# A kept score made by one VectorE operation of two inputs and turned once, in place of a ScalarE part and a VectorE part turned twice

## The reference, cut to what matters

```python
xn = _rmsnorm(x, norm_w)
q = (xn @ w_q.T).reshape(b, t, H, 2, DK)              # H = 8 heads
sim1 = jnp.einsum('bthd,hkd->bthk', q[..., 0, :], keys[:, :, 0, :])   # 32 keys
sim2 = jnp.einsum('bthd,hkd->bthk', q[..., 1, :], keys[:, :, 1, :])
...
fs, pk = jax.lax.top_k(all_sc, K)                     # the 8 best of the sums s1 + s2
hidden = jax.nn.gelu(jnp.einsum('btd,bthkd->bthk', xn, wd), approximate=False)
hidden = hidden * jax.nn.relu(fs)
return jnp.einsum('bthk,bthkd->btd', hidden, wu)
```

## Time and profile before

| | us |
|---|---|
| median of 3 runs | 3211.59 |
| lowest and highest | 3202.09, 3213.86 |
| the profiled execution | 3200.05 |
| its span, first to last instruction | 3198.3 |
| mean granted TensorE clock | 0.869 |

### The profile page before, as it was taken

How to read it: one execution, slowest core, us unless ns; L and a number is a source line. 1 busy time by engine, 2 the same in 40 slices (tenths; PEclk the granted TensorE clock), 3 DMA queues, 4 the chain that set the end, 5 groups by cost and what they waited for, 6 DMA issues and landing times.

```text
span 3198.3 us, 41256 instructions
## 1 busy us (share of the span) xinstructions
PE 2715.7 (85%) x14161; PEld 1369.0 (43%) x14161; DVE 1759.3 (55%) x4863; ACT 1373.9 (43%) x3204; POOL 602.8 (19%) x849
## 2 busy tenths in 40 slices
PE   6898998889987888888879988987899788889885
PEld 3233335334543675244423333452345347732353
DVE  5535437645654687624565444476357548776154
ACT  2545622452324543564435556225532345335741
POOL 1220001220112672000013200003201138610000
PEclk9988998988878998869779888998898689988776
DMA  4000000000000000000100000000001000000000
GB/s 168 2 1 1 1 1 25 26 2 20 29 19 1 1 27 27 1 1 31 37 8 2 1 1 1 1 26 26 1 20 33 14 1 1 27 28 1 1 1 7
DMA packets 16432, 49.71 MB, mean 16 GB/s; under 512 B 1761, under 2 KB 8801, under 8 KB 14434
## 3 DMA queue, kind: packets, MB, share of 16 engines
q1 hardware_dynamic: 15650, 45.79, 4.1%
q10 hardware_dynamic: 576, 1.29, 0.1%
HBM read 45.43 MB, written 1.05 MB: 15 GB/s over the span
## 4 chain that ended last, share of the span: by engine, by line
PE 66%; DVE 17%; ACT 9%; issue 6%; POOL 1%; DMA 0%; SPq 0%; ACTq 0%; DVEq 0%; POOLq 0%
PE psum L582 5%; PE psum L2155 4%; PE psum L995 4%; PE psum L549 4%; PE psum L572 3%; PE psum L1006 3%; DVE floor_s L2254 2%; PE psum L979 2%; PE psum L1530 2%; PE psum L1822 2%; PE psum L1360 2%; PE psum L821 2%; PE psum L746 2%; ACT PT_s L648 2%; PE psum L1818 2%
## 5 line engine op out<-in xcount | busy, mean ns | idle before, releaser
L648 ACT ACTIVATE PT_s<-psum 128x512 f32<-128x512 f32 (+3 forms) x768 | 344.9, 497 | 277.7 <-PE psum L572 276.0
L396 POOL TENSOR_SCALAR ve<-mv 128x4 f32<-128x4 f32 x48 | 13.5, 281 | 1668.9 <-DVE mv L386 1668.7
L708 DVE CUSTOM_DVE_ANT_0 rest_s<-psum,packed_early 128x128 f32<-128x128 f32 (+3 forms) x512 | 226.6, 487 | 152.2 <-PE psum L555 150.1
L2181 POOL TENSOR_TENSOR buffer<-sim_s 128x1024 f32<-128x1024 f32 x128 | 271.7, 2138 | 171.7 <-DVE floor_s L2254 86.9
L572 PE MATMUL psum<-QS_s,KS_s 64*128 64x512 bf16 (+3 forms) x768 | 199.3, 364 | 36.1 <-DVE mx_s L708 16.6
L555 PE MATMUL psum<-KS_s,QS_s 64*128 64x512 bf16 (+3 forms) x768 | 186.9, 354 | 43.2 <-DVE mx_s L711 20.1
L582 PE MATMUL psum<-PT_s,vaug 128*9 128x512 f32 (+3 forms) x1536 | 179.4, 542 | 45.3 <-POOL PT_s L681 29.4
L681 POOL TENSOR_SCALAR_AFFINE_SELECT PT_s<-PT_s 128x128 f32<-128x128 f32 x512 | 146.0, 294 | 340.3 <-ACT PT_s L648 334.8
L711 DVE TENSOR_REDUCE mx_s<-psum 128x1 f32<-128x512 f32 x256 | 161.8, 683 | 83.7 <-PE psum L555 82.9
L1043 ACT ACTIVATE PT_s<-psum 128x512 f32<-128x512 f32 (+1 forms) x224 | 121.0, 592 | 164.4 <-PE psum L997 164.3
L2214 ACT ACTIVATE above_s<-buffer,below_s 128x1024 f32<-128x1024 f32 x128 | 145.2, 1149 | 96.6 <-POOL buffer L2181 58.0
(11 more groups left out here) (446 smaller groups left out, 5382.8 us busy)
## 6 DMA issues: line engine op xcount, KB each, us to landing
buffer<-packed_experts SPq DMA_DIRECT2D x36, 384.0 KB, 3.3
buffer<-packed_moe SPq DMA_DIRECT2D x4, 2048.0 KB, 8.2
buffer<-packed_cross SPq DMA_DIRECT2D x4, 2048.0 KB, 7.9
buffer<-packed_product SPq DMA_DIRECT2D x4, 1024.0 KB, 4.9
packed_early<-packed_early SPq DMA_DIRECT2D x1, 2654.5 KB
QS_s<-nmT_s SPq DMA_DIRECT2D x144, 4.0 KB
raw_s<-packed_setup SPq DMA_DIRECT2D x1, 1840.0 KB, 7.6
packed_late<-packed_late ACTq DMA_DIRECT2D x4, 314.0 KB, 3.7
```

The source lines that it names most:

```text
L648: a.activation(PT[:, u // 4 % 2, i, q0_of(c):T], bank[u % 3][:, q0_of(c):T], ACT.Exp, scale=scale).then_inc(exp_done.sem, 1)
L708: v.tensor_tensor_reduce(junk[:, u % 2, 0:w], bank[n % 4][:, 0:w], s.w["causal"][:, T - w:T], 1.0, -3e38, ALU.add, ALU.max, mx[:, j, h:h + ...
L2181: g.tensor_tensor(fs[:, n % 2], m[:, 0, :].unsqueeze(2).to_broadcast([P, NK, NK]), m[:, 1, :].unsqueeze(1).to_broadcast([P, NK, NK]), ALU. ...
```

## The change

ACT's part and the negative threshold go. DVE makes the kept score in one `scalar_tensor_tensor`, `(sum >= threshold) * sum`, which reads the tensor of sums as both of its tensor inputs. PE turns one tile of 1024 columns with 8 transposes where it turned two with 16. The ring has three tiles in place of two times two. POOL, PE and the copy of the similarities wait for `marked` alone.

```diff
-    KEPT = 2
+    KEPT = 3
...
-    below = s.tile("below9", [P, 2, NH])
...
-    above = s.tile("above9", [P, KEPT, NK * NK])
-    floor = s.tile("floor9", [P, KEPT, NK * NK])
+    kept = s.tile("kept9", [P, KEPT, NK * NK])
...
                 yield at(j, h) + 2.4
-                pe.wait_ge(*risen(n + 1))
                 pe.wait_ge(*marked(n + 1))
...
-                for i, rows in enumerate((above, floor)):
-                    for c in range(EC):
-                        mm = pe.matmul(CT[:, c * P:(c + 1) * P], rows[:, n % KEPT, c * P:(c + 1) * P], s.w["ident"][:], is_transpose=True,
-                                       start=(h == 0 and i == 0 and c % 4 == 0), stop=(h == NH - 1 and i == 1), skip_group_check=True)
+                for c in range(EC):
+                    mm = pe.matmul(CT[:, c * P:(c + 1) * P], kept[:, n % KEPT, c * P:(c + 1) * P], s.w["ident"][:], is_transpose=True,
+                                   start=(h == 0 and c % 4 == 0), stop=(h == NH - 1), skip_group_check=True)
...
                 if n >= 2:
-                    g.wait_ge(*risen(n - 1))
                     g.wait_ge(*marked(n - 1))
...
-                yield at(j, h) + 0.4
-                total, ready = sum_of(n)
-                a.wait_ge(*ready)
-                if h == 0:
-                    a.wait_ge(*limits_ready(j + 1))
-                if n >= KEPT:
-                    a.wait_ge(*added(n - KEPT + 1))
-                a.activation(above[:, n % KEPT, :], total, ACT.Relu, bias=below[:, j % 2, h:h + 1]).then_inc(risen.sem, 1)
...
-            link(v.tensor_scalar(thr[:, j % 2, :], best[:, :, 7], 0.0, None, ALU.max))
-            v.tensor_scalar(below[:, j % 2, :], thr[:, j % 2, :], -1.0, None, ALU.mult).then_inc(limits_ready.sem, 1)
+            v.tensor_scalar(thr[:, j % 2, :], best[:, :, 7], 0.0, None, ALU.max).then_inc(limits_ready.sem, 1)
+            v.wait_ge(*limits_ready(j + 1))
...
-            v.tensor_scalar(floor[:, n % KEPT, :], total, thr[:, j % 2, h:h + 1], thr[:, j % 2, h:h + 1], ALU.is_ge, ALU.mult).then_inc(marked.sem, 1)
+            v.scalar_tensor_tensor(kept[:, n % KEPT, :], total, thr[:, j % 2, h:h + 1], total, ALU.is_ge, ALU.mult).then_inc(marked.sem, 1)
```

More of the change, by code:

```diff
@@ L2082, in l2_ffn @@
     (chain, limits_ready, squares_ready, eps_added, inv_ready, xs_ready, xs_turned, xnT_ready, hidden_ready, gelu_ready, sim_ready, sim_copied, summed,
-     risen, marked, added, weighted, out_ready) = s.signals(
-        chain=1 + 4 * TJ, limits_ready=TJ, squares_ready=1, eps_added=1, inv_ready=1, xs_ready=TJ, xs_turned=1, xnT_ready=1, hidden_ready=EC, gelu_ready=EC,
-        sim_ready=TJ, sim_copied=TJ, summed=N, risen=N, marked=N, added=N, weighted=TJ, out_ready=TJ)
+     marked, added, weighted, out_ready) = s.signals(
+        chain=1 + 3 * TJ, limits_ready=TJ, squares_ready=1, eps_added=1, inv_ready=1, xs_ready=TJ, xs_turned=1, xnT_ready=1, hidden_ready=EC, gelu_ready=EC,
+        sim_ready=TJ, sim_copied=TJ, summed=N, marked=N, added=N, weighted=TJ, out_ready=TJ)
     s.new_stage()
@@ L2191, in copy_sim @@
             if j >= 2:
-                a.wait_ge(*risen(NH * (j - 1)))
                 a.wait_ge(*marked(NH * (j - 1)))
@@ L2205, in scalar @@
             for h in range(NH):
-                n = j * NH + h
-                yield at(j, h) + 0.4
-                total, ready = sum_of(n)
-                a.wait_ge(*ready)
-                if h == 0:
-                    a.wait_ge(*limits_ready(j + 1))
-                if n >= KEPT:
-                    a.wait_ge(*added(n - KEPT + 1))
-                a.activation(above[:, n % KEPT, :], total, ACT.Relu, bias=below[:, j % 2, h:h + 1]).then_inc(risen.sem, 1)
                 if h == 1 and 1 <= j < TJ - 1:
```

## The result

| | before | after |
|---|---|---|
| median of 18 runs | 3207.78 us | 3218.24 us |
| lowest and highest | 3196.30, 3217.56 | 3211.22, 3223.49 |
| the profiled execution | 3200.05 us | 3219.69 us |
| its span | 3198.3 us | 3218.0 us |

The ratio of the changed kernel to the one before is 1.0036, with a 95% interval of 1.0024 to 1.0048: 11.5 us slower, between 8 and 15. That is within the 0.5% named in the prediction, but clear of zero. With more runs the median of before came down from 3211.59 to 3207.78, so that the forecast of 3219 was met to a microsecond by a difference of 7 that should have been 11. That closeness is luck; the difference is what counts.

The account below looks back on a forecast made before the run. Shared stretches were taken as bound by DVE and POOL excluding each other, not by PE's transposes. The terms, 2 x (15 - 8.5 - 5.0 + 2) = +7 us, took the median from 3212 to 3219 us, range 3190 to 3244.

Parts of the forecast that it names:

- forecast case: Whole kernel: the forecast's own case, median 3219 us, 3203 to 3229, chance 0.50.
- lead: Part of each turn where stream 0 makes scores alone (1016 to 1101): forecast 8.5 us shorter.
- tail: Part of each turn with scores of stream 1 alone (1166 to 1256): forecast 5.0 us shorter.
- shared stretch: Part of each turn with scores of both streams (1101 to 1166): forecast 15 us longer, PE's saving giving nothing.
- clock: PE's clock falls in the shared stretch and the tail's first products pay: +2 us a turn, between 0 and 8.
- The exclusion: Shared stretch: the two-input DVE operation holds POOL up, 0.55 us more for each of 27 sums, 15 us.
- Rival C: Slower by TensorE's clock, low through the shared stretch into the tail: 8 to 10 us a turn, 3233, chance 0.20.
- A: Lead and tail: the transposes' 58 us go in full, as DVE isn't next; -26 us, 3186, chance 0.17.
- B: The new form doesn't exclude POOL, or runs at today's rate: -45 us, 3167, chance 0.05.
- D: Shared stretch: POOL is held for all of the operation's 1.22 us, +22 a stretch; +21, 3233, chance 0.08.
- ACT, the threshold and the ring: Dropping ACT's 147 us and the negative threshold, and a ring of three: all 0 outside one lead piece.

Follow-up runs that it names:

- e8: The changed kernel with only the scores of the shared stretch turned twice, their sum doubled; 3214.12 us, ratio 1.0037 to before.
- e4: The kernel before with the two-input operation as its VectorE part, ScalarE's part and 16 transposes kept; 3246.88 us, ratio 1.0109.
- e2: The changed kernel with a one-input VectorE copy of the sums, about as long, threshold left out; 3148.64 us, ratio 0.9798 to before.
- e3: The changed kernel with each kept score turned twice, 16 transposes a score, sum doubled; 3247.01 us, ratio 1.0112 to before.
- e1: The changed kernel with the one-input operation of before, 8 transposes, the part above the threshold left out; 3168.39 us, ratio 0.9865 to before.
- e7: e5 with an accumulator output on VectorE's shared-stretch operation, which then only compares, without multiplying by the threshold; 3174.74 us, ratio 0.9899 to before.
- e6: The changed kernel with a ring of two kept tiles in place of three; 3219.66 us, ratio 1.0034 to before.
- e5: The kernel before with the changed form for scores of lead and tail, the shared stretch's made as before; 3198.56 us, ratio 0.9969.

## Why the prediction was right, point by point

The forecast case came in: no gain, since what PE saves in lead and tail is outweighed by what DVE and POOL take from each other in the shared stretch. By its own steps, for a turn:

| step | forecast | measured |
|---|---|---|
| shared stretch | +15 | +14.0 |
| lead | -8.5 | -4.3 |
| tail | -5.0 | -3.0 |
| clock | +2, carried into the tail | 0 carried over (e8); what falls inside lead and tail is in their figures |
| sum | +3.5 | +6.7 |

The forecast named 76 and 85 us as the lead and the tail to come, and 76.7 and 85.4 were measured. That is no confirmation: the forecast took its steps from the rounded stretches of 85 and 90 us, the measured ones begin at 81.0 and 88.4. The steps came out at half and at six tenths of what was forecast.

*The exclusion* was right in mechanism and size. The price of 0.55 us a sum was taken from one row of POOL beside a two-input operation; it measured 0.53. That it is the exclusion and nothing else is shown from both sides: e4 puts the operation into the kernel before and gets +14.3 with everything else kept, but for an operation that is also longer; e2 tells length and exclusion apart: it takes the exclusion out of the changed kernel and gets -28.6 with the length of the operation nearly kept. That PE's saving is worth nothing there is shown by e3, 80.0 with twice the transposes.

*The lead* was mis-sized, above all in its DVE term. The two parts of the change can be put in one after the other, in either order. First the transposes (before, e1, after): halving them with the one-input operation gives 8.2 us, and the two-input operation then takes 3.9 back. First the operation (before, e4, e3, after): it costs 6.4, and halving the transposes then gives 11.3; ScalarE's part, the threshold and the ring make up the 0.6 between e4 and e3. The forecast had 10.9 for PE's side (7.0, 0.3, 1 and 2.6) and only 2.4 for the operation, as 0.41 us for each of six that stood on the chain. That price, the operation's length alone, is the step that was too small in both orders. With 8 transposes its length is worth 0.5 (e2 against e1), and the other 3.4 is the exclusion of POOL, which the forecast counted in the shared stretch alone: the changed kernel's lead is 3.4 longer than e2's, whose operation is 0.07 shorter and excludes nothing.

The clock in the lead was not foreseen either. Timeline of PE where stream 1's last projection runs, in the changed kernel and then before:
```profile
1059.69 0.39 PE L746 MATMUL psum<-packed_late,attT_s 128*128 128x128 f32 x2
1060.01 0.79 PE L748 MATMUL psum<-packed_row,ones 1*128 1x128 f32 x2
1060.73 0.80 PE L746 MATMUL psum<-packed_late,attT_s 128*128 128x128 f32 x2
...
1064.35 0.79 PE L748 MATMUL psum<-packed_row,ones 1*128 1x128 f32 x2
```
```profile
1062.18 0.39 PE L746 MATMUL psum<-packed_late,attT_s 128*128 128x128 f32 x2
1062.50 0.48 PE L748 MATMUL psum<-packed_row,ones 1*128 1x128 f32 x2
...
1064.99 0.48 PE L748 MATMUL psum<-packed_row,ones 1*128 1x128 f32 x2
```
The eight groups take 5.4 us after the change and 3.2 before: the granted clock is 0.5 from 1060.0 for 17.1 us, where before it fell only at 1070.9, for 6.8 us. Every kernel here with 8 transposes in the lead has this fall, 36 to 38 us into it. It doesn't need the shorter transposes: e3, with 16, has the groups in 5.7 us, wholly at 0.5, after a fall 43 us into its lead. In e4, the kernel before with nothing but the new operation, the clock is 0.5 for 3.4 us at 1028.6 and again at 1062.7; two turns of 16 transposes on the chain take 2.97 and 3.10 us in place of 1.94 and 1.94, and the groups 3.8. So about 2.7 of e4's 6.4 come by the clock (an estimate: these pieces less those of before), and there it fell with nothing changed but the operation. But e1, with the one-input operation and 8 transposes, has the long fall too. Either part of the change will do, then; what decides it was not tried.

*The tail* has the mechanism named, DVE next after PE. The 8 transposes with a one-input operation give 8.0 (e1); the two-input operation takes 5.0 back, 3.2 by its length and 1.8 by the exclusion (e2 lies between the two; that e1's operation excludes POOL a little too is left out of this split). The forecast let through 7.4 and took 2.4 back, and -3.0 is what was left: again the operation's price was too small. In the other order the operation costs 0.3 (e4) and the halving gives 2.3 (e3), so the parts don't add up independently here.

*Clock.* Rival C put the slower outcome on a low clock through the shared stretch. The clock did fall in the shared stretch, to 0.68 and 0.74, under the point named in one turn; but in the tail's first 20 us it was 0.76 and 0.83 (0.91 before), not under 0.7. In the shared stretch PE was busy for 63 and 59%, where the forecast said under half. The price of the low clock in that stretch was zero, 80.0 us at 0.68 and at 0.96 alike, and e8 has 0.76 at the start of the tail as well: what C held, that the low clock is carried over, is refuted. The tail's own fall stays, inside the -3.0, with its price open.

*The other rivals.* A, the transposes' time comes through (its sum has +2 for the clock where two turns make +4, which changes nothing here): not so. Even with the one-input operation (e1) leads and tails lose 32 us in the two turns, not the 58 of this rival. B, no exclusion: refuted by POOL's 2.89. D, POOL held for the whole operation: a POOL cycle of 3.1 was its mark, and 2.86 was measured. The Trainium skill, in SBUF — State Buffer, section "SBUF: two separate sides", says that the shared pair goes to whichever operation starts first, for the whole instruction. With the measured 1.28 us that would be a cycle of 3.18; the measurement is 0.32 below it and decides. For the same reason the prediction's sentence on the earlier trace rows, that neither engine works while the other does, says too much: a part of the DVE operation does run beside POOL's. The Trainium skill also says, on the same page in "Who interferes with whom", that a VectorE instruction with at most one SBUF input, outside the two-port modes, does not contend with GpSimd. e2 and e7 agree, with POOL at 1.91 us (median) and 1.96 (mean).

*ACT, the threshold and the ring* were put at 0. e3 against e4 gives 0.1 us in the median, where PE turns 16 times (+0.6 in a lead, -1.1 in a tail), and e6 gives 0 for the ring.

## What to carry to other kernels

Where DVE and POOL work on SBUF side by side, cost a DVE operation twice: by its length on DVE, and by how long it keeps POOL out, which the trace shows as POOL operations that are longer than their shortest. Folding two one-input operations into one of two inputs saved ScalarE's pass and half of the transposes, and still lost, because the stretch where both streams meet is bound by that exclusion. When a form wins in one stretch and loses in another, and the order of the work is fixed, choose it by place: e5 keeps the gain and leaves the loss.

## What the runs showed of the hardware that was not expected

A DVE operation slower by half a microsecond made its stretch faster: 1.33 us with an accumulator against 0.81 without, and 58.3 us in place of 67.1 for the stretch, as POOL was no longer held up.

A granted clock of 0.68 through 80 us of a kernel whose TensorE is busy for 63% of them cost nothing measurable: 80.0 us at 0.68 and at 0.96.

Stretches whose code is the same in all kernels come out at one of a few lengths. Between two layer norms early in a turn the first turn of before took 92.3 us and e3 90.5, and in the second turn before and e8 took 92.1 and all others 93.7; the next two took 104.0 and 103.0 in the second turn of before and of e8, and 104.8 and 105.3 in most others. What the whole program does outside the six stretches varies so by up to 15 us (2725 to 2740) between profiled executions of these kernels. That is as much as the effect of the change, so the stretches, cut at the same instructions, tell it better than the time of one execution does. It is also why stretches and medians differ, by 2 us for the change and by some 10 for e1, e2 and e4: the profiled execution of before has only 2728 us outside, and is itself 8 below its median. What decides which length comes out was not tested.
